# Causal attention on one core: the lagged products with matrices stationary over 512 tokens, copied and turned

## The reference

```python
# attention: q, k = elu(.) + 1; running sums over the tokens
num = jnp.einsum('bti,btij->btj', q, kv_cum)
den = jnp.einsum('bti,bti->bt', q, k_cum)[..., None] + 1e-06
t = t + num / den
# lagged part of the second half, on u = layernorm(t), Mu of shape (3, 128, 128)
out = jnp.zeros(u.shape[:2] + (Mu.shape[-1],), dtype=u.dtype)
for i in range(Mu.shape[0]):
    ui = jnp.pad(u, ((0, 0), (i, 0), (0, 0)))[:, :sl]
    out = out + jnp.einsum('btd,de->bte', ui, Mu[i])
```

## Time and profile before

| | |
|---|---|
| median of 3 runs | 8973.17 us (8971.49 to 8999.93) |
| profiled execution | 8970.96 us, its span 8969.1 us |
| busy: PE, DVE, ACT, POOL | 3200.8, 6027.8, 1391.0, 4467.7 us |
| mean granted TensorE clock | 0.65 of full speed |

### The profile page before, as it was taken

How to read it: one execution, slowest core, us unless ns; L and a number is a source line. 1 busy time by engine, 2 the same in 40 slices (tenths; PEclk the granted TensorE clock), 3 DMA queues, 4 the chain that set the end, 5 groups by cost and what they waited for, 6 DMA issues and landing times. The chain is left out here.

```text
span 8969.1 us, 108428 instructions
## 1 busy us (share of the span) xinstructions
PE 3200.8 (36%) x41604; PEld 2271.7 (25%) x41604; DVE 6027.8 (67%) x8397; ACT 1391.0 (16%) x2614; POOL 4467.7 (50%) x4747
## 2 busy tenths in 40 slices
PE   4103001030011101210021002103854786999997
PEld 2001000010001100100011001102432665888884
DVE  7688786978767677978667766774633654555553
ACT  1000000000000000000000000002211332444442
POOL 0777777777777777777777777760000000000000
PEclk7556555565555555555555555556776888999998
DMA  3434445444543343434633343333035232222224
GB/s 74 135 112 128 119 124 147 119 121 120 155 117 112 109 131 111 128 109 122 160 111 112 108 132 111 112 105 60 1 112 143 64 96 75 68 65 66 66 68 187
DMA packets 822795, 966.53 MB, mean 108 GB/s; under 512 B 283016, under 2 KB 643424, under 8 KB 817760
## 3 DMA queue, kind: packets, MB, share of 16 engines
q0 software_dynamic: 221184, 604.27, 23.0%
q1 hardware_dynamic: 573744, 321.19, 14.4%
q10 hardware_dynamic: 27440, 34.87, 1.1%
HBM read 797.58 MB, written 155.99 MB: 106 GB/s over the span
## 5 line engine op out<-in xcount | busy, mean ns | idle before, releaser
L511 POOL DMA_INDIRECT l_rec<-records,l_row x4608 | 4411.5, 957 | 1619.6 <-issue 1338.7
L1051 DVE TENSOR_TENSOR l_rec<-l_rec,l_psv 128x2304 f32<-128x2304 f32 x256 | 653.9, 2554 | 1291.5 <-DMA l_rec<-records,l_row 1289.6
L2323 DVE COPY l3p_mix<-l3p_ps 128x512 f32<-128x512 f32 x1024 | 660.0, 686 | 577.9 <-PE l3p_ps L2199 577.9
L1070 DVE TENSOR_REDUCE l_att_t<-l_rec 128x64 f32<-128x2304 f32 x256 | 1027.4, 4013 | 8.8
L780 ACT ACTIVATE l_prob<-l_score 128x18 f32<-128x18 f32 x256 | 55.8, 218 | 5472.2 <-DVE l_score L1056 5472.2
L678 PE MATMUL l_pso<-l_id,l_att_t 128*128 128x128 f32 x128 | 58.7, 459 | 2283.1 <-DVE l_att_t L1070 2282.9
L668 PE MATMUL l_pso<-l_wo,l_att_c 128*128 128x128 f32 x256 | 101.8, 501 | 1855.0 <-ACT l_att_c L769 1855.0
L1052 DVE TENSOR_REDUCE l_psv<-l_rec 128x72 f32<-128x2304 f32 x256 | 655.6, 2561 | 8.8
L2285 ACT ACTIVATE l3p_mix<-l3p_ps 128x512 f32<-128x512 f32 x1024 | 557.1, 596 | 663.9 <-PE l3p_ps L2199 663.9
L1068 DVE TENSOR_TENSOR l_rec<-l_rec,l_psv 128x2304 f32<-128x2304 f32 x256 | 653.6, 2553 | 8.8
L2199 PE MATMUL l3p_ps<-l3p_psi,l3p_ms 32*128 32x128 f32 x16384 | 611.4, 283 | 21.2 <-DVE l3p_mix L2323 16.7
(11 more groups left out here) (364 smaller groups left out, 6191.7 us busy)
## 6 DMA issues: line engine op xcount, KB each, us to landing
l_rec<-records,l_row POOLq DMA_INDIRECT x4608, 2.7
l2b_w<-l_w SPq DMA_DIRECT2D x32, 1024.0 KB, 10.4
records<-l_area SPq DMA_DIRECT2D x48, 512.0 KB, 10.2
l_row<-meta SPq DMA_DIRECT2D x124, 154.0 KB, 2.5
l_x_hat<-l3a_xout ACTq DMA_DIRECT2D x32, 512.0 KB, 3.8
l3p_xin<-l_x_hat SPq DMA_DIRECT2D x128, 128.0 KB, 3.1
l_y_raw<-l3p_yr SPq DMA_DIRECT2D x64, 256.0 KB, 3.5
l3p_yin<-l_y_raw SPq DMA_DIRECT2D x128, 128.0 KB, 3.0
```

Of the source, the lines that this page charges most:

```text
L511: pool.indirect_dma_start(out=rec[:, r, k, :], out_offset=None, in_=records[b].rearrange("r c d -> r (c d)"), in_offset=bass.IndirectOffse ...
L1051: step(dve.tensor_tensor(keys, keys, asked.broadcast_to([P, HG, TAPS * CORNERS, HC]), ALU.mult))
L1070: step(dve.tensor_reduce(att_t[two][:, HG * HC * h:HG * HC * (h + 1)].rearrange("p (g d) -> p g d", g=HG), values.rearrange("p g m d -> p ...
L2323: dve.tensor_copy(mix[t.side(0)][:, x:x + 2, :, :].rearrange("p x c e -> p (x c e)"), ps[(2 * q + h) % 3][:, 1, :]).then_inc(s_setd, 1)
```

## The change

The lagged matrices become the stationary side. A job `ar` is now three products, each with one lagged matrix stationary and 512 tokens of `chans` moving: 6 passes of 512 columns. Its result is channel-major. ScalarE, no longer VectorE, reads it and copies it to `lags_c`, a name for the tile `state`, which is free at that time. Eight new jobs `at` follow the eight `ar`: each turns four pieces of 128 columns back to token-major by TensorE, and `lagged(b)` on VectorE now waits for these.

```diff
+        lags_c = state[:, :, :].rearrange("p t c -> p (t c)")[:, 0:N]
...
-            return [(kind, b, g, "dve" if kind in ("a", "s", "ar") else "act") for g in range(n)]
+            return [(kind, b, g, "dve" if kind in ("a", "s", "at") else "act") for g in range(n)]
...
-            jobs += part_of("u2", b) + part_of("ar", b)
+            jobs += part_of("u2", b) + part_of("ar", b) + part_of("at", b)
...
                 if kind == "ar":
+                    for lag in range(LAGS):
+                        i = 2 + g * 512 - lag
+                        last = pe.matmul(bank[:, :], mats_u[:, lag, :], chans[b % 2][:, i:i + 512], start=lag == 0, stop=lag == LAGS - 1)
+                if kind == "at":
+                    pe.wait_ge(s_act, taken(AT["ar", b, g], "act"))
                     for t in range(4):
-                        for lag in range(LAGS):
-                            i = 2 + (4 * g + t) * P - lag
-                            last = pe.matmul(bank[:, t * P:t * P + P], chans[b % 2][:, i:i + P], mats_u[:, lag, :],
-                                             start=lag == 0, stop=lag == LAGS - 1)
+                        i = (4 * g + t) * P
+                        last = pe.transpose(bank[:, t * P:t * P + P], lags_c[:, i:i + P], id_s[:, :])
...
+                if kind == "ar":
+                    if g == 0:
+                        act.wait_ge(s_two, b + 1)
+                    ins = act.activation(lags_c[:, cols], bank[:, :], ACT.Copy)
...
-                    n = AT["ar", b, g]
+                    n = AT["at", b, g]
                     dve.wait_ge(s_job, n + 1)
```

## The result

The changed kernel took 9013.22 us (median of 6 runs, 9010.60 to 9017.58), the kernel before beside it 8972.33 (6 runs, 8971.03 to 8999.93): ratio 1.0041, interval [1.0028, 1.0054], 41 us slower. On another chip, beside the experiments, it took 9002.23 against 8975.19: ratio 1.0034, interval [1.0023, 1.0045], 27 us by the medians and 30 by the ratio. The forecast was 9024, slower.

What follows compares the result with a forecast made beforehand. PE was taken to bound `lagged`, with VectorE's work under it. Paced `k` 19.2, clock in `v` 22.5 and last batch 11.5 gave +53 us on 8970.96, so 9024; own range 9012 to 9030, with the second case 8996 to 9033.

Steps and rivals of the forecast that it cites:

- PE's part: PE in `lagged`: long passes 20.7 us instead of 21.68, plus transposes 3.7; in sum +2.9 us a batch.
- ScalarE's part: Eight copies of 512 columns, about 0.7 us each, lie in ScalarE's idle time after the exponential; cost 0.
- VectorE's uncovered part: Masks and adds in `lagged` lose their cover: 1.68 us a bank, `lagged` ends 11.5 us later.
- `k` paced: VectorE's 1.68 us a bank holds back `k`; PE 6.4 us later at `f` and `v`, three times: 19.2 us.
- The last batch: Token store, last pieces for `f` and spectral stage move by VectorE's whole 11.5 us; bounds 11 to 12.
- The clock in `v`: Clock falls to half 0.8 us into `v` in batches 1 to 3, making `v` longer: 22.5 us in all.
- the half-used stretch: PE work in `k` at 0.87 of every 1.68 us, from about 7062.5; clock falls a median 10 us later.
- The spectral row: Spectral stage: PE works 1.17 of 2.07 us; after 6.2 us the same passes take 2.09.
- One of the step's bounds: Clock in `v`: 13 us less in sum if it falls 14 us after the half-used stretch starts, so 12.
- The rival that left the clock alone: Gaps of 0.8 us in `k` are harmless, `v` keeps its times: 19.2 + 11.5 = 31 us, 9002; chance 27%.
- SP's chain: Token store, load of batch b+2 and last pieces for `f` move 11.5 us in batches 0 to 2; cost 0.

Runs made afterwards that it cites:

- a kernel with `k` at full pace: Kernel before plus 16 extra statistics instructions on VectorE at the head of `two(b)`: 8996.80 us against 8972.21, one run.
- full-row runs: Bias product in `v` on all 128 rows instead of one: kernel before so changed 9776.83 us, changed kernel so changed 9815.37, both against 9809.86.

## Why the prediction was right, and where it was wrong

The direction and the range held; in the stage itself the sum was 53 us against 31 measured, and one term of the three was wrong. Point by point, by the prediction's own terms:

- *PE's part*: +2.9 us a batch expected. Measured 20.67 us from `ar` to the transposes and 3.49 from these to `k`, 24.16 instead of 21.52: +2.6. Right.
- *ScalarE's part*: nothing expected, nothing found in the changed kernel.
- *VectorE's uncovered part*: right in kind and a little too large. An add is followed by the next mask after 0.72 us, not 0.84, so a bank costs 1.57 us, not 1.68. `lagged` ends 10.5 us later relative to `u2`, expected 11.5.
- *`k` paced*: 6.4 us a batch expected, 5.65 found at `f` (41.0 against 35.35), 5.5 in the two later batches: 16.6 us of the 19.2.
- *The last batch*: 11.5 expected; the store came 11.1 us later relative to the store of normalized tokens before it, but PE's wait for `xin` shrank from 20.09 to 18.48 us, and counted from the same point the spectral part begins 8.5 us later. 16.6 + 8.5 is the 25 us by which the stage without `v` grew.
- *The clock in `v`*: **the step that failed.** 22.5 us were expected, because the fall was to be counted from the start of the half-used stretch, `k` now included. The fall came 9.6, 5.7 and 5.5 us after the start of `v`, not 0.8; `v` took 23.6, 27.1 and 27.3 us in batches 1 to 3, not 31, and grew by 6.1 us in sum (105.2 - 99.1). Even these 6 are not shown to be the pace of `k`: a kernel with `k` at full pace has the same falls or earlier ones. The spectral row on which the step rested has passes of 32 rows in it, and the full-row runs show that full-array passes with gaps before `v` don't bring the fall by themselves. One of the step's bounds was also added up wrongly: a fall 14 us after the start of `k` would come 4.7 us into `v`, 3.9 later than the forecast's, which at 1.87 us per 2.14 in three batches is 10 us less, not 13.
- *The rival that left the clock alone* (31 us, 9002) was nearer, and 27 to 30 us is what the second chip shows. That its 31 are met in the stage is in part luck: its two terms of 19.2 and 11.5 measured 16.6 and 8.5, and the 6 us of `v`, which it put at nothing, fill the gap.
- *SP's chain*: nothing expected, nothing found while `v` is long; 12.75 and 12.94 us come out of it in batches 1 and 2 when `v` is short.

So of the 53 forecast 31 were measured in the stage, 25 of them without `v`. That 9013 lies inside the forecast's own range (9012 to 9030) is luck: it is owed to the 10 us outside the stage, which the second chip doesn't show.

The ratio of the Trainium skill for long against short passes (TensorE: Matmul & The Clock Gate, "Back-to-back issue gap") doesn't hold for these float32 products: 20.67 us against 21.52 for the same columns. The advice of the same page of the Trainium skill against idle gaps of some microseconds between bursts ("Why this matters for your kernels") agrees with full-row `v` at full clock after a `k` with gaps of 0.44 us; it says nothing of the fall in `v`, where there is no gap.

## What to carry to other kernels

When a producer is the bound and the consumer works in its shadow, a second pass over all results (make all, then turn all) takes the shadow away. The consumer's tail then stands alone, here 1.57 us for each of eight banks, and what of it reaches the end depends on what queues behind it: here it was 10 of the 25 us, and interleaving the two passes gave these back. The other 15, the second pass itself, stayed in either order. A wider moving side is worth only the overhead that the narrow one really shows; read it from the spacing of the passes in the trace before paying for a transposition. And a product of one row by 512 columns is no cheap way to add a bias: with all 128 rows in its place the stage of the kernel before was 27 us shorter, about as much as the change costs.

## What the runs showed of the hardware

- A float32 product of one row with 512 columns is slower than one with 128 rows, both at full clock: with one row the four short products start 1.05 us after the bias product (7065.37 and 7066.42 in the kernel before), with 128 rows 0.86 (7876.27 and 7877.13), two passes each. The four short products are quicker behind it too, 0.89 us to the next bias product against 1.09.
- In all 40 `v` stages with one-row passes (ten profiles) the full clock was lost 1 to 12 us after the start though PE was never idle; with 128 rows in their place it never was, in twelve stages. The moment of the fall was the same to 0.1 us in two profiles of one program, and moved with a few microseconds of delay ahead of it.
- 128-column and 512-column float32 passes cost 0.112 and 0.43 us in a stream of weight loads and products, 4% apart per column.
- Behind a rest of 3.85 us, after 7.4 us of dense passes at full clock, PE worked at a granted clock of 0.51 (the kernel with the bias on VectorE); behind rests of 0.44 us in `k` it stayed at 1.00.
